# One core, a four-layer network: how the input rows of the third feed-forward are selected on TensorE, and in which order ranks, products and turns are issued

## The reference, cut to what matters

```python
# L2_ffn, called with x of (64, 32, 256); SKIP = 0.125, so k = 4
logits = (x @ Wr + br)[..., 0]
weights, idx = jax.lax.top_k(logits, k)
perm = jnp.argsort(idx, axis=1)
tokens = jnp.take_along_axis(idx, perm, axis=1)
fx = jnp.take_along_axis(x, tokens[..., None], axis=1)
h = jax.nn.gelu(fx @ W1 + b1, approximate=False)
out_l = h @ W2 + b2
tw = jax.nn.softmax(weights, axis=1)
rw = jnp.take_along_axis(tw, perm, axis=1)
xw = rw[..., None] * out_l
return x.at[bidx, tokens].add(xw)
```

## Time and profile before

| what | us |
|---|---|
| median of 3 runs | 962.8 |
| the three runs | 959.43, 962.8, 963.14 |
| the profiled execution | 958.42 |
| span in its trace | 956.6 |
| busy PE / DVE / POOL / ACT in the span | 839.4 / 567.4 / 380.4 / 347.1 |
| the stage, from the end of the last copy to `ytok` to the first product of the fourth layer | 621.6 to 671.0 |

### The profile page before, as it was taken

How to read it: one execution, slowest core, us unless ns; L and a number is a source line. 1 busy time by engine, 2 the same in 40 slices (tenths; PEclk the granted TensorE clock), 3 DMA queues, 4 the chain that set the end, 5 groups by cost and what they waited for, 6 DMA issues and landing times.

```text
span 956.6 us, 16539 instructions
## 1 busy us (share of the span) xinstructions
PE 839.4 (88%) x5239; PEld 680.0 (71%) x5239; DVE 567.4 (59%) x1659; ACT 347.1 (36%) x1007; POOL 380.4 (40%) x405
## 2 busy tenths in 40 slices
PE   1999998985899999695489989979989979999997
PEld 1787776754798998684378868867447747777786
DVE  5646888555487876279487979451553444444343
ACT  3333443433233333022376868402442222221311
POOL 7300436266466677766535540000175003334000
PEclk9999999987799999798598999959998989999999
DMA  9225112777877542824788875000523003331222
GB/s 355 64 105 160 50 41 79 305 223 210 227 203 233 165 130 66 336 96 120 155 168 180 161 167 210 2 1 1 181 101 129 24 17 93 105 103 58 89 85 91
DMA packets 68179, 126.43 MB, mean 132 GB/s; under 512 B 20224, under 2 KB 50265, under 8 KB 65455
## 3 DMA queue, kind: packets, MB, share of 16 engines
q1 hardware_dynamic: 46783, 75.49, 26.2%
q0 software_dynamic: 20800, 47.76, 18.0%
q10 hardware_dynamic: 512, 2.13, 1.0%
HBM read 87.39 MB, written 43.30 MB: 137 GB/s over the span
## 4 chain that ended last, share of the span: by engine, by line
PE 61%; DMA 16%; DVE 9%; issue 4%; ACT 4%; POOL 3%; SPq 3%; DVEq 0%; POOLq 0%; ACTq 0%
PE ps L470 18%; PE ps L807 11%; PE ps L838 7%; PE ps L817 3%; DMA big<-big 2%; DMA early<-newblk,new_i 2%; DMA big<-mid 2%; DMA early<-early 2%; PE ps L2277 2%; PE ps L828 2%; PE ps L2514 2%; PE ps L2559 1%; POOL sent_d L909 1%; PE ps L2410 1%; PE ps L2453 1%
## 5 line engine op out<-in xcount | busy, mean ns | idle before, releaser
L909 POOL DMA_INDIRECT sent_d<-mid,slot_i x88 | 98.0, 1113 | 114.3 <-DVE mid L629 64.6
L851 ACT ACTIVATE early<-ps 128x256 f32<-128x256 f32 x134 | 51.3, 384 | 176.5 <-PE ps L817 176.5
L838 PE MATMUL ps<-early 96*128 (+1 forms) x346 | 99.3, 388 | 0.2
L869 DVE TENSOR_TENSOR early<-early,ps 128x96 f32<-128x96 f32 (+1 forms) x134 | 37.3, 278 | 99.5 <-ACT early L857 79.5
L900 POOL DMA_INDIRECT back_d<-early,mid x78 | 77.5, 993 | 34.6 <-issue 27.6
L504 DVE TENSOR_TENSOR hidl<-work,hidh 128x512 fp32r<-128x512 f32 (+1 forms) x56 | 38.8, 692 | 84.5 <-ACT hidh L497 84.5
L807 PE MATMUL ps<-big,early 128*128 x380 | 82.0, 339 | 3.3 <-issue 1.9
L510 ACT ACTIVATE work<-ps 128x512 f32<-128x512 f32 (+1 forms) x56 | 33.4, 596 | 138.6 <-PE ps L470 138.4
L900 POOL DMA_INDIRECT back_d<-big,mid x39 | 38.4, 984 | 111.8 <-DVE big L883 105.9
L807 PEld LDWEIGHTS ps<-big,early 128*128 128x128 f32 x380 | 69.6, 198 | 10.5 <-issue 5.2
L838 PEld LDWEIGHTS ps<-early 96*128 96x128 f32 (+1 forms) x346 | 56.2, 194 | 3.8 <-issue 1.3
(11 more groups left out here) (440 smaller groups left out, 2096.0 us busy)
## 6 DMA issues: line engine op xcount, KB each, us to landing
mid<-sent_d SPq DMA_DIRECT2D x117, 130.0 KB
big<-back_d SPq DMA_DIRECT2D x8, 512.0 KB
mid<-back_d SPq DMA_DIRECT2D x8, 512.0 KB, 7.0
early<-back_d SPq DMA_DIRECT2D x16, 256.0 KB, 3.1
early<-in_w SPq DMA_DIRECT2D x3, 1024.0 KB, 11.8
big<-in_gate SPq DMA_DIRECT2D x1, 3072.0 KB, 11.0
big<-in_up SPq DMA_DIRECT2D x1, 3072.0 KB, 16.2
early<-in_gu SPq DMA_DIRECT2D x1, 2816.0 KB, 10.0
```

The costliest lines, as they stand in the source:

```text
L838: last = nc.tensor.matmul(ps[:, 6 + j % 2, 0:D], L.hTb[j % len(L.hTb)][0:f1 - f0, h * P:(h + 1) * P], L.down[0:f1 - f0, h, bass.ds(owners[ ...
L851: nc.scalar.activation(L.yTb[b % ring_y], ps[:, b % 2, 0:2 * P], ACT.Copy).then_inc(s["turn_sb"], 1)
L869: nc.vector.tensor_tensor(L.hb[j % ring_h], L.sgb[j % 2], ps[:, 2 + j % 2, F:2 * F], ALU.mult)\
L909: nc.gpsimd.indirect_dma_start(out=sent_d, out_offset=bass.IndirectOffsetOnAxis(ap=L.slot_i[:, i:i + 1], axis=0), in_=L.rows[c][:, t, n, : ...
```

## The change

`pick` is gone. The ranks are computed by a function `rank_half(j)` on 8 tiles at a time, and each half writes its zeros and ones straight into `own_picks`, so into `pickw`; the weight is multiplied in later, in place, after TensorE has used the zeros and ones (wait for `fx_ps` 2).

TensorE's product is the other way round: `pickw` is loaded (128x64 for a tile) and the tile's rows of 256 values move, summed over the 4 tiles of a chunk. Even chunks write partitions 0 to 63, odd ones 64 to 127; the half j of the ranks gives `picked[:, j, :]`, 128 selected rows of 256 values. ScalarE copies each half (`picked_out`), TensorE turns it with two turns (`picked_turns`), and ScalarE copies `fx`.

Between, 23 products whose result nobody reads are issued (`run_warm`): the 128x128 identity as weights, 512 columns of another constant moving, both bf16, 8 of them ahead of the `lrow` product and 15 behind it. `mixed_turns(2)` and `mixed_turns(3)` both stand behind the new products, chunk 3 first. VectorE's first addition `mixed(0)` is moved ahead of the softmax. Two banks swap roles (`HALF_BANK`).

```diff
         Y0_BANK = (0, 4, 4, 4)
-        MIX, FIN, MIXED_AT = (4, 6, 2, 4), (6, 4, 2, 6), (2, 4, 3, 4)
+        HALF_BANK = (1, 0)
+        MIX, FIN, MIX_ORDER, MIXED_AT = (4, 6, 2, 4), (6, 4, 2, 6), (0, 1, 3, 2), (2, 3, 4, 4)
...
+            def picked_out(j):
+                act.wait_ge(s["fx_ps"], j + 1)
+                nc.scalar.activation(picked[:, j, :], ps[:, 1 + j, 0:D], ACT.Copy).then_inc(s["fx_sb"], 1)
+
+            picked_out(0)
             act.wait_ge(s["lex_ready"], 1)
             nc.scalar.activation(lexe, lex, ACT.Exp).then_inc(s["lexe_ready"], 1)
-            act.wait_ge(s["fx_ps"], 1)
-            nc.scalar.activation(fx, ps[:, 1, :].rearrange("p (d n) -> p d n", d=KD), ACT.Copy).then_inc(s["fx_sb"], 1)
+            picked_out(1)
+            act.wait_ge(s["fx_ps"], 3)
+            nc.scalar.activation(fx, ps[:, 0, :].rearrange("p (d n) -> p d n", d=KD), ACT.Copy).then_inc(s["fx_sb"], 1)
...
-            ch.link(nc.vector.tensor_tensor(routed[1], lrow, const(C["own"]), ALU.mult))
-            ch.link(nc.vector.tensor_reduce(lcol[:, 2, :], routed[1], X, ALU.add))
...
+            def rank_half(j):
+                i = slice(j * NT // 2, (j + 1) * NT // 2)
...
+                ch.link(nc.vector.tensor_tensor(routed[1][:, i, :], lrow[:, i, :], same(C["own"]), ALU.mult))
+                ch.link(nc.vector.tensor_reduce(lcol[:, 2, i], routed[1][:, i, :], X, ALU.add))
+                nc.vector.tensor_tensor(routed[2][:, i, :], lrow[:, i, :], each(2), ALU.is_gt)
...
+                nc.vector.tensor_tensor(own_picks[:, i, :], ranked[:, i, :], same(C["place"], PPT), ALU.mult)\
+                    .then_inc(s["pick_ready"], 1)
...
+            rank_half(0)
+            rank_half(1)
...
+            mixed(0)
             dve.wait_ge(s["lexe_ready"], 1)
...
+            dve.wait_ge(s["fx_ps"], 2)
+            nc.vector.tensor_tensor(own_picks, own_picks, over(lcol[:, 6, :], PPT), ALU.mult)\
+                .then_inc(s["pickw_ready"], 1)
+            for c in MIX_ORDER[1:]:
                 mixed(c)
...
+            def run_warm(bank, count):
+                for _ in range(count):
+                    nc.tensor.matmul(ps[:, bank, :], identb[:, :], tselb[:, 0:512 // P, :], start=True, stop=True)
+
...
-            mixed_turns(2)
-            pe.wait_ge(s["pick_ready"], 1)
-            for i in range(NT):
-                for d in range(KD):
-                    last = nc.tensor.matmul(ps[:, 1, d * D + i * PPT:d * D + (i + 1) * PPT],
-                                            ytok[:, i, d * P:(d + 1) * P], pick[:, i, :], start=True, stop=True)
-            last.then_inc(s["fx_ps"], 1)
+            run_warm(1, 15)
+            for j in range(2):
+                pe.wait_ge(s["pick_ready"], j + 1)
+                for c in (2 * j, 2 * j + 1):
+                    for t in range(TPC):
+                        last = nc.tensor.matmul(ps[c % 2 * CHP:(c % 2 + 1) * CHP, 1 + j, 0:D],
+                                                pickw[:, c, t * CHP:(t + 1) * CHP], ytok[:, c * TPC + t, :],
+                                                start=(t == 0), stop=(t == TPC - 1))
+                last.then_inc(s["fx_ps"], 1)
+
+            def picked_turns(j):
+                pe.wait_ge(s["fx_sb"], j + 1)
+                for d in range(KD):
+                    last = nc.tensor.transpose(ps[:, 0, d * D + j * P:d * D + (j + 1) * P],
+                                               picked[:, j, d * P:(d + 1) * P], ident)
+                if j == 1:
+                    last.then_inc(s["fx_ps"], 1)
+
+            pe.wait_ge(s["lex_ready"], 1)
+            picked_turns(0)
+            mixed_turns(3)
+            picked_turns(1)
+            mixed_turns(2)
             pe.wait_ge(s["pickw_ready"], 1)
...
-            mixed_turns(3)
```

More of the change, by code:

```diff
@@ L327, in build @@
         routed = [early[:, ROW + j * CH:ROW + (j + 1) * CH].rearrange("p (i e) -> p i e", i=NT) for j in range(5)]
[L328 to L329 removed]
+        ranked = early[:, 6656:6656 + NT * PPT].rearrange("p (i n) -> p i n", i=NT)
         lcol = early[:, 7168:7296].rearrange("p (a i) -> p a i", i=NT)
@@ L1454, in _ @@
                 for m in (2 * j, 2 * j + 1):
-                    last = nc.scalar.activation(hT2[:, m, :], ps[:, j % 2, m % 2 * D:(m % 2 + 1) * D], ACT.Gelu,
+                    last = nc.scalar.activation(hT2[:, m, :], ps[:, HALF_BANK[j % 2], m % 2 * D:(m % 2 + 1) * D], ACT.Gelu,
                                                 bias=b21[:, m:m + 1])
@@ L2023, in _, with same, each @@
[L2023 to L2027, removed]
+            def rank_half(j):
+                i = slice(j * NT // 2, (j + 1) * NT // 2)
+                def same(x, n=S):
+                    return x[:, 0:n].unsqueeze(1).broadcast_to([P, NT // 2, n])
+                def each(x, n=S):
+                    return lcol[:, x, i].unsqueeze(2).broadcast_to([P, NT // 2, n])
+                ch.link(nc.vector.tensor_tensor(routed[1][:, i, :], lrow[:, i, :], same(C["own"]), ALU.mult))
+                ch.link(nc.vector.tensor_reduce(lcol[:, 2, i], routed[1][:, i, :], X, ALU.add))
+                nc.vector.tensor_tensor(routed[2][:, i, :], lrow[:, i, :], each(2), ALU.is_gt)
+                ch.link(nc.vector.tensor_tensor(routed[3][:, i, :], lrow[:, i, :], each(2), ALU.is_equal))
+                ch.link(nc.vector.tensor_tensor(routed[4][:, i, :], routed[3][:, i, :], same(C["before"]), ALU.mult))
+                ch.link(nc.vector.tensor_tensor(routed[3][:, i, :], routed[4][:, i, :], routed[2][:, i, :], ALU.add))
+                ch.link(nc.vector.tensor_reduce(lcol[:, 3, i], routed[3][:, i, :], X, ALU.add))
+                ch.link(nc.vector.tensor_tensor(ranked[:, i, :], same(C["rank"], PPT), each(3, PPT), ALU.is_equal))
+                if j == 0:
+                    dve.wait_ge(s["qzero"], 2)
+                nc.vector.tensor_tensor(own_picks[:, i, :], ranked[:, i, :], same(C["place"], PPT), ALU.mult)\
+                    .then_inc(s["pick_ready"], 1)
@@ L2028, in _, with mixed @@
+            def mixed(c):
+                dve.wait_ge(s["turned2"], MIX_ORDER.index(c) + 1)
+                for d in range(KD):
+                    cols = xT[:, d, c * CH:(c + 1) * CH]
+                    last = nc.vector.tensor_tensor(cols, ps[:, MIX[c] + d, :], cols, ALU.add)
+                last.then_inc(s["mixed"], 1)
+            rank_half(0)
+            rank_half(1)
             for i in range(NT):
@@ L2052, in _ @@
                 dve.wait_ge(s["acc_ready"], NCH + c + 1)
-                dve.wait_ge(s["mixed"], c + 1)
+                dve.wait_ge(s["mixed"], MIX_ORDER.index(c) + 1)
                 for d in range(KD):
@@ L2472, in _ @@
                 for k in range(KD):
-                    last = nc.tensor.matmul(ps[:, m // 2 % 2, m % 2 * D:(m % 2 + 1) * D], w21[:, k, m * P:(m + 1) * P],
-                                            fx[:, k, :], start=(k == 0), stop=(k == KD - 1))
+                    last = nc.tensor.matmul(ps[:, HALF_BANK[m // 2 % 2], m % 2 * D:(m % 2 + 1) * D],
+                                            w21[:, k, m * P:(m + 1) * P], fx[:, k, :], start=(k == 0), stop=(k == KD - 1))
                 if m % 2 == 1:
                     last.then_inc(s["h_ps"], 1)
-            mixed_turns(3)
             for j in range(2):
```

31 lines of the change are left out of this document (12 added, 19 removed).

## The result

| | before | changed |
|---|---|---|
| median of 4 runs | 961.12 us | 946.33 us |
| lowest and highest | 952.5, 963.14 | 941.66, 948.83 |
| profiled execution | 958.42 us | 948.83 us |
| its span | 956.6 us | 947.0 us |

The ratio is 0.9886 with a 95% interval of 0.9841 to 0.9932: faster by 0.7% to 1.6% (the quotient of the two medians is 0.985, inside the interval). The forecast for the median was 952.4 us, with a range of 947.5 to 958.0. As a difference the forecast was 10.4 us, and the interval is 6.6 to 15.3 us. The two profiled executions are 9.6 us apart.

A forecast was written before the change was run, and what follows sets the result against it. The stage's chain, one engine at a time, was the bound, with TensorE's clock at 0.50 through the selection. Terms -0.6 - 2.1 - 7.6 + 2.7 - 1.9 - 0.9 = -10.4 us took 962.8 to 952.4 us; range 947.5 to 958.0.

The forecast's parts named there:

- `lrow`: TensorE's product ahead of the ranks: 512 columns moved twice at full clock, 0.9 us in place of 1.54, -0.6 us.
- ranks, up to the first selection: VectorE's ranks in halves: the first half is there after 3.7 us in place of 5.9, -2.1 us.
- selection, first to last: TensorE's 32 instructions at full clock with overlapping array halves: 6.2 us in place of 13.8, -7.6 us.
- turns behind it: 20 turns behind the selection, 2.4 us, plus a 0.3 us wait: +2.7 us new in the chain.
- `pickw`: Turning of pickw on TensorE at clock 1.00: 2.1 us taken in place of 4.01, -1.9 us.
- turns ahead of the second product: mixed_turns(3) leaves its place between the products L2473 and L2483: -0.9 us.
- stage: The part the diff touches, slice 27's clock dip; its terms sum to -10.4 us, reaching the kernel's end.
- the pause ahead of the selection: TensorE's idle time between the end of the 15 unread products and the first half of the ranks: 0.55 us.
- The first rival: Array halves don't overlap at full clock: half a selection 3.5 us, -8.4 us in all, 954.4 us; chance 0.24.
- The second: TensorE's clock falls in the new pauses ahead of and inside the selection: 956 to 959.4 us; chance 0.10.
- The wait of 0.3 us for `mixed(0)`: Before chunk 3's turns, TensorE arrives at 635.3 and waits for VectorE's addition, done at 635.5: 0.3 us.
- the change of tiling mode: One added pair of switches from 128 weight columns to 64 and back; the engine drain adds nothing to the sum.

The follow-up runs named there:

- the run on one side: The changed kernel with the odd chunks' selection written to the same partitions 0 to 63 as the even ones': stage 40.3 us.
- the version with hidden turns: Changed kernel with even and odd chunks alternating, VectorE's first addition before its lrow wait, turns of chunks 2 and 3 behind lrow: stage 37.2 us, ratio 0.9897.
- The run with unread products alone: The kernel before plus 8 unread products ahead of lrow and 22 behind chunk 2's turns, old selection kept: stage 45.8 us, ratio 0.9989.

## Why the prediction was right

| step | forecast | measured |
|---|---|---|
| `lrow` | -0.6 | 1.54 to 1.16: -0.4 |
| ranks, up to the first selection | -2.1 | 5.88 to 3.75: -2.1 |
| selection, first to last | -7.6 | 13.83 to 6.5: -7.4 |
| turns behind it | +2.7 | +2.4 |
| `pickw` | -1.9 | 4.01 to 2.50: -1.5 |
| turns ahead of the second product | -0.9 | -0.9 |
| stage | -10.4 | -9.8 |

The mechanism held step by step: the clock, the release of the ranks after 3.75 us (3.7 forecast) and 7.3 us, the pause ahead of the selection (0.55) and the overlap of the array's halves. The first rival (no overlap, 3.5 us a half) is refuted at 2.86, and by the run on one side. The second (the clock falls in the pauses) did not happen: it stayed at 1.00 over pauses of 0.55 and 0.75 us, and over 1.65 us in the version with hidden turns.

What was off in size: a half of the selection is 2.86 us, not 2.5 to 2.6, because I took 1.0 us for a border from L2461 and set its 4.01 us against 7.0 at clock 0.50, though its last 0.8 us ran at 1.00, as I had written myself. Counted twice, those make 4.8 us at 0.50, so three borders saved 2.2, 0.73 each, and 3.5 - 0.73 = 2.8 us is what a half takes. The run with unread products alone has L2461's form at 0.50 throughout, and there it takes 4.64 us up to the next product (670.62 to 675.26). For the same reason `pickw` is 2.50, not 2.0 to 2.1. `lrow` takes 1.16 us in the chain and not 0.9: TensorE starts its next product 0.96 us after it (622.35 to 623.31), which is what I had priced, but VectorE starts only at 623.51. The wait of 0.3 us for `mixed(0)` wasn't there: VectorE was done 10.4 us after the `lrow` product, as forecast, but TensorE, with the longer selection, got there only then.

I had put the change of tiling mode (from 128 weight columns to 64 and back) at nothing, since the chain showed no gap. But a product's end is modelled, and by the starts there is a price:

```profile
633.35 0.38 PE L2484 MATMUL ps<-early,work 128*64 128x256 f32 x1
633.66 0.33 PE L2492 MATMUL ps<-late,big 128*128 128x128 f32 x1
```

From the selection's last product to the first turn it is 0.31 us, where the products of a run start every 0.22 us and a border at which the weights keep their 128 columns (L2434 to L2462, 618.36 to 618.57) shows 0.22 as well (L2434 makes attention's last rows, L2462 is the first turn). The two added borders thus cost some 0.1 us each, small beside the sum.

What I argued but had not separated: the text gives the clock back to the removal of the idle time ("they take away the idle time behind which the clock fell") and to the selection together. The runs show that the idle time could have stayed. With the old selection, full clock at its start was lost 4.6 us in; with the new one, the clock came back by itself within 3.1 to 4.9 us. Without the unread products the stage would be at most 0.55 us longer in the two executions seen. The prediction was right in that the clock would hold, and gave the unread products a part in it that the new selection did not need. What in the turned-round selection brings the clock back, no run separates. I had also counted -2.1 us for the ranks in halves. The term is real at the place where I put it, but 1.8 of it is given back as the pause between the halves and a border less, so that leaving the halves out costs only 0.3 us of the stage.

The median of the changed runs lies below the range. The stage did what was forecast within 0.6 us; what was mis-sized is the scatter around it. I had set the lower end from the fastest of four executions (958.4), and the fourth timed run of the kernel before was at 952.5. What moves between executions shows behind the stage, in the same instructions of the fourth layer's first expert block (L807). Windows of TensorE at one place of it, before and then changed:

```profile
785.00:788.00 3.00, 2.33 (x10) 0.98 0.19 47
```

```profile
773.00:776.00 3.00, 2.78 (x6) 0.50 0.19 47
...
779.00:779.50 0.50, 0.50 (x5) 1.00 0.00 0
```

Both lie at the same place, 114 us behind the stage's end (671.0 and 659.4); the instruction there starts at 785.27 before and at 773.22 changed. The clock was back just ahead of it in one execution (785.1), and in the other only at 779.0, some 6 us later in the work, with the same waits in front. At this place the changed kernel is 12.05 us ahead; at 789.28 and 779.68, the same instruction again, it is 9.6 us ahead, as at the end. So 2.4 us were lost here. The changed kernel's other trace, whose instruction at this place starts at 818.79, has the clock back in time, so the loss does not belong to the change:

```profile
819.00:822.00 3.00, 2.60 (x11) 1.00 0.28 62
```

## What to carry to other kernels

Ask of a run of small 32-bit products which operand is loaded and which moves: loading the selection and moving the rows made 13.8 us into 6.5. With it the clock came back by itself in all three runs in which it had fallen ahead of the selection, while unread products ahead of the old form did not keep it. If there are only 64 weight columns, put neighbouring products on different halves of the array, alternating one by one (1.95 us for 16 instructions, 2.86 in runs of eight, 3.6 on one side). Before adding unread products look for real work to put there, and measure each part of a bundle by leaving it out: here four fifths of the gain are one part (the turned-round selection with its order of turns), and the other two mostly stand in for each other.

## What the runs showed of the hardware that I had not expected

- TensorE busy without a gap is not enough to keep its clock: it fell 4.6 us into the selection (L2460) of the run with unread products alone, and stayed at 0.50 for the 13.8 us of L2453. The Trainium skill, in its page TensorE: Matmul & The Clock Gate, in the part on the HAM clock gate, says that the gate is set by how busy the engine has been recently; by the profile's busy time these rows disagree.
- The pairs of column halves overlap as the page TensorEngine Tiling (Array Packing) of the Trainium skill has it in Key Properties; it gives "Up to 2×" in Theoretical Speedup, and the runs show 3.6 to 1.95 us, a factor of 1.9. Key Properties also says that a change of tiling mode drains the engine, without a figure. The trace agrees that there is a price, of about 0.1 us a border: 0.31 us between the starts at 633.35 and 633.66 in place of 0.22.
- How late TensorE's clock comes back after a pause differed by some 6 us between two executions of equal work, at the same place of the program (785.1 before and 779.0 changed, where the same instruction starts at 785.27 and 773.22).
